# First feed-forward of a two-layer AdaLN megakernel: 80 router and low-rank columns projected in plain fp32

## What is computed

```
h = layernorm(x) * (1 + cb) + sb
base_out   = h @ base_w.T + base_b            # 512 columns
res_hidden = h @ A.T                          # low-rank, R = 64 columns
logits     = h @ router_w.T                   # E = 16 columns
probs = softmax(logits); topw, topi = top_k(probs, 2)
topw  = topw / (sum(topw) + 1e-6)
combine = sum over the two of one_hot(topi) * topw
delta = einsum('bse,bsr,eor->bso', combine, res_hidden, B)
x = x + gb * (base_out + delta * 0.5)
```

## Time and profile before

| | |
|---|---|
| three runs | 1057.2 us median, 1054.76 to 1059.08 |
| profiled execution | 1052.17 us, span 1050.4 us, mean granted clock 0.93 |
| busy over the span | TensorE 860.5 us (82%), VectorE 773.3 (74%), ScalarE 530.0 (50%), GpSimd 523.1 (50%) |
| blocks, about | modulation and first attention to 182 us, first feed-forward to 297, then layer 1 |

### The profile page before, as it was taken

The page is one execution under the profiler, slowest core; times in us unless marked ns, Lnnn a source line. Parts: engine busy times, 40 slices in busy tenths (PEclk is TensorE's granted clock), DMA queues, the critical chain, the costliest instruction groups (busy, mean ns, idle before and its releaser), DMA issues. The chain is left out here.

```text
span 1050.4 us, 15116 instructions
## 1 busy us (share of the span) xinstructions
PE 860.5 (82%) x4552; PEld 566.8 (54%) x4552; DVE 773.3 (74%) x1588; ACT 530.0 (50%) x1142; POOL 523.1 (50%) x449
## 2 busy tenths in 40 slices
PE   5588884799978946899999898987999999985477
PEld 1567663677776724555555555553555554543145
DVE  1669997755535527789898989899989898982453
ACT  2277773633216724556555655554555555552143
POOL 2043332012200025787877888875787878772003
PEclk9989997699969968799999999998999999998679
DMA  9420000800026731455555555553555555555101
GB/s 331 162 107 2 2 2 2 290 1 1 1 80 241 257 84 41 110 122 123 121 128 121 123 122 125 123 124 88 125 124 124 120 126 123 124 123 118 55 11 70
DMA packets 73105, 112.29 MB, mean 107 GB/s; under 512 B 18816, under 2 KB 23936, under 8 KB 72768
## 3 DMA queue, kind: packets, MB, share of 16 engines
q1 hardware_dynamic: 60736, 94.54, 32.9%
q10 hardware_dynamic: 12288, 16.79, 6.7%
HBM read 42.06 MB, written 2.10 MB: 42 GB/s over the span
## 5 line engine op out<-in xcount | busy, mean ns | idle before, releaser
L1351 DVE TENSOR_REDUCE nmax<-bank 128x1 f32<-128x512 f32 x256 | 174.0, 680 | 55.2 <-PE bank L1291 53.1
L1426 ACT ACTIVATE prob<-bank,nmax 128x512 f32<-128x512 f32 x172 | 118.5, 689 | 170.8 <-DVE nmax L1351 170.8
L1485 POOL TENSOR_TENSOR prob<-prob,rinv 128x512 f32<-128x512 f32 x129 | 133.8, 1044 | 51.8 <-DVE rinv L1358 51.8
L1289 PE MATMUL bank<-xk_hi,q_hi 128*128 128x512 f32 x256 | 110.8, 433 | 15.2 <-ACT prob L1426 12.2
L1366 DVE STREAM_TRANSPOSE blk<-prob 128x512 f32<-128x512 f32 x172 | 120.9, 703 | 3.1 <-ACT prob L1441 0.4
L1480 POOL TENSOR_TENSOR q_lo<-stage_a,q_hi 128x512 fp32r<-128x512 f32 x64 | 82.4, 1287 | 53.7 <-ACT q_hi L1420 53.7
L1290 PE MATMUL bank<-xk_lo,q_hi 128*128 128x512 f32 x256 | 102.8, 401 | 0.0
L1291 PE MATMUL bank<-xk_hi,q_lo 128*128 128x512 f32 x256 | 101.5, 397 | 0.0
L1426 ACT ACTIVATE stage_a<-bank,nmax 128x512 f32<-128x512 f32 x84 | 57.9, 689 | 75.6 <-DVE nmax L1351 75.6
L1289 PEld LDWEIGHTS bank<-xk_hi,q_hi 128*128 128x128 f32 x256 | 49.1, 192 | 78.7 <-issue 33.0
L1476 POOL TENSOR_TENSOR stage_a<-stage_a 128x512 f32<-128x512 f32 x64 | 82.9, 1296 | 6.3 <-DVE stage_a L1346 6.3
(11 more groups left out here) (217 smaller groups left out, 2154.8 us busy)
## 6 DMA issues: line engine op xcount, KB each, us to landing
pT<-blk SPq DMA_DIRECT2D x384, 64.0 KB, 2.0
raw_e<-blk SPq DMA_DIRECT2D x384, 64.0 KB, 2.0
wmod<-in_wmod SPq DMA_DIRECT2D x12, 1024.0 KB, 11.7
raw_e<-in_wo SPq DMA_DIRECT2D x8, 1024.0 KB, 6.4
pT<-blk ACTq DMA_DIRECT2D x128, 64.0 KB, 2.1
raw_e<-blk ACTq DMA_DIRECT2D x128, 64.0 KB, 2.2
wqn<-in_wqn SPq DMA_DIRECT2D x8, 512.0 KB, 4.1
stage_a<-in_wqkv SPq DMA_DIRECT2D x4, 768.0 KB, 9.0
```

Source lines behind the costliest of these rows:

```text
L1289: pe.matmul(sbk, q_hi[:, u % 2, q], xk_hi[:, 2, ks], start=True, stop=False)
L1351: dve.tensor_reduce(nmax[:, s % RING:s % RING + 1], s_bank[s % 2][:, :], AX.X, ALU.max, negate=True).then_inc(max_done, 1)
L1426: act.activation(prob[s % RING], s_bank[s % 2][:, :], ACT.Exp, bias=nmax[:, s % RING:s % RING + 1], accum_out=rsum[:, s % RING:s % RING + ...
L1485: pool.tensor_tensor(prob[s % RING], prob[s % RING], bc(rinv[:, s % RING:s % RING + 1], [P, S]), ALU.mult).then_inc(norm_pool, 1)
```

## The change

The 80 columns of router and low-rank projection are no longer split. They are loaded once more from DRAM into a plain fp32 tile `wr` (the first transfer of the block on SyncE), and TensorE multiplies them with the unsplit fp32 `f`: one matmul call per chunk instead of three. `wf_hi` and `wf_lo` become 512 columns wide, and so do the copies and subtractions that make them. TensorE waits for hf instead of lo ahead of these matmuls, for wr_in once, and for lo ahead of the 512 columns. Since TensorE now reads f, ScalarE waits for the router part of tile t before it writes f of tile t+1.

```diff
-            wf_hi = sb("wf_hi", [P, KC, PROJ0], F32R, ph)
-            wf_lo = sb("wf_lo", [P, KC, PROJ0], F32R, ph)
+            wf_hi = sb("wf_hi", [P, KC, D], F32R, ph)
+            wf_lo = sb("wf_lo", [P, KC, D], F32R, ph)
+            wr = sb("wr", [P, KC, R0 + E0], F32, ph)
+            wr_in = sem("wr_in")
...
-            parts = ([(raw_f[:, k, :], wf_hi[:, k, :], wf_lo[:, k, :]) for k in range(KC)]
+            parts = ([(raw_f[:, k, 0:D], wf_hi[:, k, :], wf_lo[:, k, :]) for k in range(KC)]
...
                 def _(sp):
+                    sp.dma_start(wr[:, :, :], fsrc[:, :, D:PROJ0]).then_inc(wr_in, 16)
                     sp.dma_start(biasf[:, :], bc(a["bffn0"], [P, D])).then_inc(bias_in, 16)
...
                         if t + 1 < TILES:
+                            act.wait_ge(base_ps, 2 * t + 1)
                             nrm.act_h(act, t + 1, pT)
...
                     def project(t):
-                        pe.wait_ge(nrm.lo, t + 1)
+                        pe.wait_ge(nrm.hf, t + 1)
+                        if t == 0:
+                            pe.wait_ge(wr_in, 16)
                         if t >= 2:
                             pe.wait_ge(z_done, t - 1)
-                        split_matmuls(pe, r_bank[t % 2][:, 0:R0 + E0], [
-                            (nrm.h(t, c), (wf_hi[:, c, D:PROJ0], wf_lo[:, c, D:PROJ0]))
-                            for c in range(KC)]).then_inc(base_ps, 1)
+                        for c in range(KC):
+                            mm = pe.matmul(r_bank[t % 2][:, 0:R0 + E0], nrm.f[:, c, :], wr[:, c, :],
+                                           start=(c == 0), stop=(c == KC - 1))
+                        mm.then_inc(base_ps, 1)
+                        pe.wait_ge(nrm.lo, t + 1)
                         if t >= 2:
                             pe.wait_ge(fsum_done, t - 1)
```

## The result

| | before | changed |
|---|---|---|
| median, 12 runs each | 1053.69 us (1051.34 to 1059.08) | 1049.99 us (1044.76 to 1052.47) |
| ratio, 95% interval | | 0.9955, 0.9935 to 0.9976 |
| the same once more, below | 1053.22 us | 1049.18 us, 0.9961, 0.9942 to 0.9979 |
| profiled execution's span | 1050.4 us | 1050.7 us |

The changed kernel is 0.4% faster: 3.7 and 4.0 us by the medians, 4.7 and 4.1 us by the ratios (which aren't the quotients of the medians), where 3.3 was forecast. The interval leaves 1 out, and I had said that a measurement would hardly tell the gain from nothing.

What follows compares the result with a forecast made beforehand. TensorE, always busy, was taken to bound the changed block. Router 7 x 0.43 = 3.0 us plus narrower splits 0.3 us gave 3.3 us: 1057.2 - 3.3 = 1053.9 us, range 1049.8 to 1058.2.

Steps and rivals of the forecast that it cites:

- What bounds the block, and the price of an instruction: First feed-forward block: TensorE always busy; fp32 call is two instructions of 0.114 us, gaining 0.43 us per tile.
- the rival of four loads: Router matmuls: each fp32 call makes four passes with own loads, 1.82 us per tile, time 1060.3; chance 0.03.
- The upper price of 0.117: Router matmuls: upper bound per fp32 instruction in us, from a second run of L364, giving 0.40 us gain per tile.
- Tile 0 hidden: Block start: tile 0's projection gains nothing, as TensorE stands until z at 199.91; only the other seven tiles count, 3.0 us.
- The new wait: ScalarE's norm of the next tile starts 0.7 us later; z's cover shrinks from 3.25 to 2.1 us; cost nothing.
- the new transfer: Block start, SP's queue: one 160 KB DMA put first, landing at 185.5 or 190.1 us; costs nothing either way.
- Narrower splits at the start: Block start: ScalarE's four copies go from 592 to 512 columns, 0.08 us each, 0.3 us, all reaching TensorE's restart.
- the judgment of what can be told: Whole kernel: measurement can tell about 0.5%, 5.3 us, from no change; 0.84 given to a result within that.
- The clock rival: Behind tile 0: longer TensorE idle keeps the clock low through tile 1, 6.4 us more, time 1060.3; chance 0.05.
- one of my signs of being wrong: Changed profile, TensorE's clock: the forecast is wrong if the stretch after 203 us is at 0.50.
- the next one starts at 296.58 and not near 294.1: Block end: a sign of the forecast being right was the next block starting near 294.1 us, where it was 297.41.

Runs made afterwards that it cites:

- router_twice: Changed kernel with the four fp32 router calls made twice in each tile; ratio 1.0005, block 116.98 us, tile period 12.502 us.
- before_512: Kernel before, its twelve split router matmuls reading tiles of their own, wf in rows of 512; tile period 12.058 us, block 114.08 us.
- row_592: Changed kernel with wf_hi and wf_lo declared 592 columns wide, only 512 written and read; tile period 11.746 us, block 111.71 us.

## Why the forecast came out as it did

*What bounds the block, and the price of an instruction: right.* TensorE is never idle between tile 1 and the last tile. Going from twelve split to eight fp32 instructions is worth 0.42 us a tile with wf rows of 592 and 0.45 with rows of 512, against 0.43 forecast, and router_twice has 0.112 us each where 0.114 was taken from another block's matmuls. Two instructions per fp32 call, and one load each (64 matmul and 64 load records for 32 calls): the rival of four loads is out. The upper price of 0.117 came from a row of L364 that holds one step of 0.170 at the clock's rise; its other steps are 0.112 or 0.111.

*Tile 0 hidden: right.* The start gained 0.2 us where 0.3 were forecast; I had read 0.61 us per copy from a merged row that includes its last one's full length (the starts are 0.59 apart before, 0.52 after).

*The new wait, the new transfer: nothing, right.* The wait was confirmed by taking it away, and its cover by using it up. The transfer showed no wait of TensorE's; it wasn't tried alone.

*The failed step is "Narrower splits at the start", taken for all that the narrower wf does.* The term stood at 0.3 us for the copies alone, and the wide matmuls were left at their old spacing without a reason. The narrower wf also shortens the rows that they read, and that takes 0.11 to 0.14 us off each period (before_512, row_592), 0.8 to 1.0 us over seven tiles. So the narrower wf is worth 1.0 to 1.2 us and not 0.3. With it the sum is 0.2 + 7 x 0.56 = 4.15 us, and the medians say 3.7 and 4.0.

*The second is the judgment of what can be told.* I took 0.5% as the least visible difference and gave 0.84 to no telling difference. Twelve runs of each kernel give an interval of 0.2% to each side, and a gain of 3.3 us, 0.31%, already stood outside that. The time itself, 1049.99, is in the range only at its lower end, by 0.2 us; that is luck, also because the three runs shown had a median of 1057.2 where the nine that followed them have 1052.85.

*The clock rival* had its condition and about a tenth of its price. Tile 0's projection ended 1.9 us earlier and not 1.2 (it starts at hf instead of lo, has four matmuls fewer, and the clock rose sooner), so TensorE stood 4.6 us where nearly 4 were worked out, and the clock came back 4.6 us after the restart instead of 3.3. That costs 0.6 us: 13.81 us to tile 1's z where 13.24 are seen when it comes back after 3.4. Read by the letter, one of my signs of being wrong came true, the stretch from 203 to 206 us is at 0.50; the block began 2.7 us later in this execution, and for the same reason the next one starts at 296.58 and not near 294.1.

No run shows the longer low clock to be the change's doing. In five executions with the split router and the old order the clock came back 3.2, 3.3, 7.6, 9.4 and 9.4 us after the restart, in ten with the fp32 router after 2.8 to 4.6. If the change has an effect on it, it is the opposite of the rival's, and the gain is above 4.15 us: three blocks with the kernel before's work last 114.85 to 117.57 us, six with the changed kernel's 110.42 to 111.42. Whether that is chance or the change isn't shown.

## What to carry to other kernels

Where narrow matmuls (64 to 128 columns behind a 128x128 load) fill an engine that is never idle, count instructions: one costs 0.11 us here whether it is split or fp32, and plain fp32 makes two of three. When an operand no longer needs its split, look at what that lets start earlier: the order of the block's start was worth more (6.7 us on top, and 4.5 to 6 in the kernel before) than the arithmetic. And judge a change of this size by a stretch of the profile that repeats to 0.01 us, with the clock's share of it set apart, rather than by two spans.

## What was not expected of the hardware

The spacing of full-length matmuls changed with the row length of a tile that only a third of them read. With wf rows of 592 elements, 36 matmuls in a row take 8.22 to 8.25 us, with rows of 512 they take 8.10 to 8.12, in all kernels of the table, and the 24 expert matmuls, which don't read wf, have the slow spacing too (0.2333 against 0.2289 us) when they follow the wide projection. In tile 7, where no projection is ahead of them, they run at 0.229 even in the kernel before (288.01 to 292.59 us, 20 steps). It looks as if the pace that the first twelve fall into is kept until the stream breaks; that is a reading of these rows and wasn't tested, and why a row of 592 (or what begins elsewhere with it) sets the slower one was not found out.
